# Loading half of the first adjacency block ahead of the class labels in a two-layer graph kernel

## The chip, the cores and the metric

The kernel runs on one core of one Trainium2 chip. The metric is the device time of one execution in microseconds (us). Five engines work side by side and meet through semaphores: TensorE (PE, matrix multiply; PEld is its weight load), VectorE (DVE), ScalarE (ACT), GpSimd (POOL) and SyncE (SP), which here only issues DMAs. Each engine runs its own instructions in order.

## The reference

There are 5000 nodes with 128 features, a symmetric 0/1 adjacency matrix `adj` (5000 x 5000, f32, 100 MB) and one-hot class labels `y` (5000 x 16). Two layers follow, each with a residual and a layer norm:

```
A1   = adj * (y @ y.T);  A1 = A1 / max(row sum of |A1|, 1e-12)
x    = layernorm(x + 0.9 * (A1 @ x) + 0.1 * h0)
sim  = tanh(adj * adj) * (adj > 0);  keep the 350 largest of each row
h2   = tanh(x @ W_proj + b_proj)
x    = layernorm(x + relu(kept @ (h2 @ W_gcn) + b_gcn))
```

So the first layer averages each node's neighbours of the same class. In the second layer every kept entry is tanh(1), as long as no row has more than 350 ones.

## The kernel before

`packed_path` holds the work; `general_path` is a second version that runs only when the data break the first one's assumptions. The 5000 rows are cut into 40 blocks of 128 (the last has 8). Block `t` of `adj` is loaded once, in two halves `h` of 2688 and 2312 columns, into `a_rows[par][h]` (par = t % 2, so two blocks in flight). Each half goes two ways:

- VectorE casts it to 0/1 in bf16 (`cast`, L777, into `a_bits`). TensorE multiplies the bits by powers of two (`pack_rows`, L464), which makes 16-bit words of 16 rows each and turns the block on the way. ScalarE copies the words to `a_words` (L695).
- ScalarE counts its zeros (`count_zeros`, L672), an activation that sums over the row. The counts are for the test of the assumptions at the end.

A half may be overwritten when both are done (SyncE's waits in `load_rows`, L332 and L333). From step 2 on, loads wait for that.

The labels make "words of the same class": ScalarE and VectorE each cast y (L647, L789) and mask it (L649, L791), TensorE transposes (L479) and packs (L488), the results are copied into a block-diagonal form (L655, L797), and `gram_words` (L497) multiplies them. Eight products are made per group, copied into `g_words` by ScalarE and VectorE in turn (`copy_gram`, L317). Then `mask` (L885) takes the AND of a block's adjacency words and class words, `unpack` (L858) spreads the bits into fp8 weights (`turned`), and `multiply` (L527) forms their product with x, which is split into a high and a low f16 part (`high_part` on ScalarE, `low_part` on VectorE). This is the first layer for one block; its norm, projection and `h2 @ W_gcn` follow some steps later, in the same loop.

The loop over blocks is a software pipeline: step t casts, counts and packs block t, masks and unpacks t-1, multiplies t-2, and finishes t-3 to t-7. The first 13 steps are written out; step 0 and 1 have their own order (`first_step`, L950). After the loop over all blocks a second loop multiplies the stored words with the features of the second layer. No `adj` is loaded then.

The order of the start, which the change touches: SyncE issues y in three parts (L350, L351, and L353 after `s_cleared`, a clear by VectorE), then both halves of block 0 (L354), x in six parts, block 1, and the rest. All are on one queue. ScalarE's first data is y (L645), then the diagonal copies and its share of class words; its first count is in step 0 (L715), ahead of the words of block 0 and the high parts of x. VectorE's first data is y (L786); its first cast (L800) comes behind the diagonal copies.

Of the kernel before, what the change touches and what calls it, by code (L numbers as in the profile page):

```python
# [6 lines left out]
P = 128  # L7
# [11 lines left out]
ACT = mybir.ActivationFunctionType  # L19
# [13 lines left out]
HUGE = 2.0 ** 63  # L33
# [3 lines left out]
def packed_path(nc, engines, sem, x, adj, h0, y, w_proj, b_proj, w_gcn, b_gcn, out, flag, s_flag, s_out):  # L37
# [13 lines left out]
    HALF = [slice(0, HB * P), slice(HB * P, N)]  # L51
# [78 lines left out]
    def valid(b):  # L130
        return not isinstance(b, int) or 0 <= b < NB

    with ExitStack() as ctx:
# [158 lines left out]
        def pairs_of(a, lo, hi):  # L292
            return a[lo * P:hi * P, :].rearrange("(s p e) f -> p s (e f)", p=P, e=2)

        def pair_view(t, lo, hi):
            return t[:, lo:hi, :].rearrange("p (s e) f -> p s (e f)", e=2)
# [26 lines left out]

        @engines.sync
        def _(sp):
            def load_rows(t, par, pair):
                if not valid(t):
                    return
                m = rows_of(t)
                for h in range(2):  # L330
                    if not isinstance(t, int) or t >= 2:
                        sp.wait_ge(s_bits, t * 2 - 3 + h)  # L332
                        sp.wait_ge(s_counted, t * 2 - 3 + h)  # L333
                    sp.dma_start(a_rows[par][h][0:m, 0:HALF[h].stop - HALF[h].start],
                                 rows_in(adj, t, par, pair, HALF[h])).then_inc(s_rows[par][h], 16)

            def load_h0(n, par, pair, i, c):

                slot, _ = h0_group(i, c)
                if not isinstance(n, int) or n >= 3:  # L340
                    sp.wait_ge(s_xh, n - 2)
                if isinstance(n, int) and n in (0, LAST):
                    m = rows_of(n)
                    sp.dma_start(h0_rows[slot][0:m, 0, :], rows_in(h0, n, par, pair, slice(0, F))).then_inc(s_h0[slot], 16)
                else:
                    both = h0[P:FULL * P, :].rearrange("(s p e) f -> s p (e f)", p=P, e=2)
                    both = both[pair] if isinstance(n, int) else both[bass.ds(pair, 1), :, :].rearrange("a p c -> p (a c)")
                    sp.dma_start(h0_rows[slot][:, :, :].rearrange("p e f -> p (e f)"), both).then_inc(s_h0[slot], 16)

            sp.dma_start(pair_view(y_nat, 1, FULL), pairs_of(y, 1, FULL)).then_inc(s_in["y"], 16)  # L350
            sp.dma_start(y_nat[:, 0, :], y[0:P, :]).then_inc(s_in["y"], 16)  # L351
            sp.wait_ge(s_cleared, 1)
            sp.dma_start(y_nat[0:TAIL, FULL, :], y[FULL * P:N, :]).then_inc(s_in["yt"], 16)  # L353
            load_rows(0, 0, 0)  # L354
            sp.dma_start(xs[:, 0, :], x[0:P, :]).then_inc(s_in["x0"], 16)
            for q, part in enumerate(X_PART):
                lo, hi = max(part.start, 1), min(part.stop, FULL)
                sp.dma_start(pair_view(xs, lo, hi), pairs_of(x, lo, hi)).then_inc(s_in[f"x{q}"], 16)
            sp.dma_start(xs[0:TAIL, FULL, :], x[FULL * P:N, :]).then_inc(s_in["xt"], 16)
            load_rows(1, 1, 0)  # L360
            load_h0(0, 0, 0, 0, 0)
            load_h0(1, 1, 0, 0, 1)
            sp.dma_start(wp[:, :], w_proj).then_inc(s_in["wp"], 16)
            sp.dma_start(wg[:, :], w_gcn).then_inc(s_in["wg"], 16)
            sp.dma_start(bp_col[:, :], b_proj.rearrange("(p a) -> p a", a=1)).then_inc(s_in["bp"], 16)
            sp.dma_start(bg_row[:, :], b_gcn.rearrange("(a p) -> a p", a=1)).then_inc(s_in["bg"], 16)

            def step(t, par, pair, i, c):
                if not isinstance(t, int) or t >= 2:
                    load_rows(t, par, pair)  # L370
                if valid(t - 1) and c >= 4 and par == 0:
                    load_h0(t - 1, 1, pair - 1, i, c - 1)
            steps4(sp, step, 4, 5)

            def store(t, par, pair):
                m = rows_of(t)
                sp.wait_ge(s_result, t + 1)
                sp.dma_start(rows_in(out, t, par, pair, slice(0, F)), xn[par][0:m, :]).then_inc(s_out[par], 16)
            steps(sp, store, 0)
# [260 lines left out]
        def _(act):  # L640
            act.wait_ge(s_const, 3)
            act.activation(tanh1, ones[:, 0:1], ACT.Tanh).then_inc(s_tanh1, 1)
            act.wait_ge(s_cleared, 2)

            act.wait_ge(s_in["y"], 32)  # L645
            act.wait_ge(s_in["yt"], 16)
            act.activation(y2[:, :, C:2 * C], y_nat[:, :, :], ACT.Copy).then_inc(s_y2, 1)  # L647
# [20 lines left out]
            for g in range(GRAMS):  # L668
                if not gram_on_dve(g):
                    copy_words(g)  # L670

            def count_zeros(t, par, pair, h, m):  # L672


                act.wait_ge(s_rows[par][h], pair * 16 + 16)
                w = HALF[h].stop - HALF[h].start
                col = zeros_in[0:m, bass.ds(t * 2 + h, 1)]
                act.wait_ge(s_counted, t * 2 + h)
                act.activation(count_out[0:m, 0:w], a_rows[par][h][0:m, 0:w], ACT.Relu,  # L679
                               bias=ones[0:m, 0:1], scale=-HUGE,  # L680
                               accum_out=col).then_inc(s_counted, 1)

            def measure(parts, sums, h, n):

# [5 lines left out]
            def step(t, par, pair):  # L690
                odd = (par + 1) % 2

                def words_of(n, par):

                    act.wait_ge(s_packed, n * 2 + 2)  # L695
                    act.activation(at(a_words, n, P).rearrange("p (b w) -> p b w", w=PITCH)[:, :, 0:WORDS + 1],  # L696
                                   words[par][:, 0:NB * PITCH].rearrange("p (b w) -> p b w", w=PITCH)[:, :, 0:WORDS + 1],
                                   ACT.Copy).then_inc(s_words, 1)

                if valid(t - 1) and not (isinstance(t, int) and t <= 1):  # L700
                    words_of(t - 1, odd)
                if isinstance(t, int) and t >= 1:
                    for g in gram_of_step(t - 1):
                        if not gram_on_dve(g):
                            copy_words(g)
                if valid(t - 6):
                    m6 = rows_of(t - 6)
                    act.wait_ge(s_in["bp"], 16)
                    act.wait_ge(s_proj, t - 5)
                    if not isinstance(t, int) or t >= 7:  # L710
                        act.wait_ge(s_feat, t - 6)
                    act.activation(h2_t[:, 0:m6], proj_acc[:, 0:m6], ACT.Tanh, bias=bp_col[:, :])\  # L712
                        .then_inc(s_h2, 1)
                if valid(t):
                    count_zeros(t, par, pair, 0, rows_of(t))  # L715
                if isinstance(t, int) and t == 0:
                    words_of(0, 0)
                    high_part(0)
                    high_part(1)
                    copy_words(GRAMS)  # L720
                    high_part(2)
                    copy_words(GRAMS + 2)
                    high_part(3)
                    copy_words(GRAMS + 4)
                if valid(t - 5):
                    m5 = rows_of(t - 5)
                    act.wait_ge(s_xnt, t - 4)
                    if not isinstance(t, int) or t >= 6:
                        act.wait_ge(s_proj, t - 5)
                    act.activation(xn_t[:, 0:m5], xnt_acc[:, 0:m5], ACT.Copy).then_inc(s_xnt_sb, 1)  # L730
                if valid(t):
                    count_zeros(t, par, pair, 1, rows_of(t))
                if isinstance(t, int) and t == 1:
                    for g in range(2 * GRAMS, 3 * GRAMS):
                        if not gram_on_dve(g):
                            copy_words(g)
                if valid(t - 6):
                    act.wait_ge(s_feat, t - 5)
                    if isinstance(t, int) and t == 6:
                        act.wait_ge(s_cleared, 3)  # L740
                    act.activation(at_cols(f_parts, t - 6, m6, 0, F), feat_acc[0:m6, 0:F], ACT.Copy,
                                   scale=SCALE)\
                        .then_inc(s_high, 1)
# [16 lines left out]
        def _(dve):  # L760
# [16 lines left out]
            def cast(t, par, pair, h):  # L777
# [3 lines left out]
                if not isinstance(t, int) or t >= 1:  # L781
                    dve.wait_ge(s_packed, t * 2 - 1 + h)
                dve.tensor_scalar(a_bits[h][0:m, 0:w], a_rows[par][h][0:m, 0:w], 1.0, None,  # L783
                                  ALU.is_equal).then_inc(s_bits, 1)

            dve.wait_ge(s_in["y"], 32)  # L786
            dve.wait_ge(s_in["yt"], 16)
            dve.wait_ge(s_cleared, 2)
# [7 lines left out]
            for g in range(TURN):  # L796
                dve.tensor_copy(y_diag[g * 2 * C:(g + 1) * 2 * C, Y_PACK[0], g, :],  # L797
                                y_pack[0].rearrange("p (r w) -> p r w", w=GRAM_W)).then_inc(s_yp_sb, 1)

            cast(0, 0, 0, 0)  # L800

            def copy_words(g):
                copy_gram(dve.tensor_copy, dve, g)
# [747 lines left out]
```

## Time and profile before

| | |
|---|---|
| median of 3 runs | 467.72 us (467.58 to 469.69) |
| profiled execution, its own time | 467.99 us |
| its span, first to last instruction | 466.2 us |
| PE / PEld / DVE / ACT / POOL busy | 94 / 83 / 81 / 57 / 34% |
| moved by DMA | 108.50 MB, nearly all before 262 us |

The span is cut into instructions of each engine; a row of a timeline gives start and length, the engine, the line of the program, what is written and read, and in brackets the idle time before it and what ended it. Names such as `a_rows<-in_adj_dram` are out<-in. A DMA is issued by SyncE (SPq, the time there is that of the issue alone) and lands later. The busy share of an engine is an average; only the waits tell what sets the end.

### The profile page before, as it was taken

Reading aid. Unit: us, or ns where it says so; the run is one execution under the profiler, and the core shown is the slowest. Engines: PE = TensorE matmul, PEld = TensorE weight load, DVE = VectorE, ACT = ScalarE, POOL = GpSimd, SP = SyncE. Lnnn points to the kernel's source line nnn. Section 1 sums busy time; section 2 is a strip of 40 time slices with the busy share of each in tenths; the row PEclk is TensorE's granted clock in tenths of the full one; section 3 lists DMA queues with packets and bytes.
Section 4 is the critical chain, followed back from the end, with each engine's and each line's share of the span. In section 5 each row is a group of like instructions: output and inputs, shape, how many; then the busy total and the mean of one; then the engine's idle time right before and its main releaser. Section 6 shows DMA issues by size and latency. Waiting matters only on the chain.

```text
span 466.2 us, 15130 instructions
## 1 busy us (share of the span) xinstructions
PE 437.5 (94%) x5104; PEld 387.8 (83%) x5104; DVE 377.8 (81%) x1358; ACT 263.8 (57%) x355; POOL 160.0 (34%) x310
## 2 busy tenths in 40 slices
PE   3669999999999999999999999999999999999994
PEld 2448988888888988888888887888888888888883
DVE  5988999999999999999999976675576576576562
ACT  4997998989999999999999934900000000000000
POOL 3012543555444455544445541221211221221222
PEclk9987999999999999999999999999999999999999
DMA  8999999999999999999999200000000000000000
GB/s 263 409 414 423 420 419 415 405 389 413 417 419 426 422 422 412 421 424 416 423 417 426 63 2 1 13 11 17 17 11 17 17 11 17 17 11 17 17 12 23
DMA packets 25518, 108.50 MB, mean 233 GB/s; under 512 B 5097, under 2 KB 15490, under 8 KB 15490
## 3 DMA queue, kind: packets, MB, share of 16 engines
q1 hardware_dynamic: 25490, 108.14, 57.4%
q8 instruction: 16, 0.26, 0.2%
q14 instruction: 12, 0.10, 0.1%
HBM read 105.57 MB, written 2.56 MB: 232 GB/s over the span
## 4 chain that ended last, share of the span: by engine, by line
PE 75%; DVE 11%; issue 6%; ACT 5%; DMA 2%; POOL 1%; DVEq 0%; POOLq 0%; SPq 0%; ACTq 0%
PE acc L522 64%; PE words L472 6%; DVE a_bits L783 3%; DMA a_rows<-in_adj_dram 2%; DVE turned L870 2%; PE feat_acc L585 2%; PE proj_acc L596 2%; ACT count_out L679 2%; ACT count_out L686 2%; PE xnt_acc L577 1%; DVE g_words L320 1%; ACT count_out L755 1%; DVE z_high L921 1%; ACT count_out L747 1%; DVE same_class L893 1%
## 5 line engine op out<-in xcount | busy, mean ns | idle before, releaser
L522 PE MATMUL acc<-x_parts,turned 128*128 128x257 f16 (+1 forms) x1600 | 192.9, 277 | 4.8 <-DVE turned L870 3.8
L679 ACT ACTIVATE count_out<-a_rows,ones 128x2688 bf16<-128x2688 f32 (+1 forms) x80 | 190.1, 2377 | 0.5
L522 PEld LDWEIGHTS acc<-x_parts,turned 128*128 128x128 fp8e4 (+1 forms) x1600 | 155.1, 99 | 28.1 <-issue 5.2
L522 PE MATMUL acc<-f_parts,turned 128*128 128x256 f16 (+1 forms) x1560 | 171.6, 273 | 0.8 <-DVE turned L870 0.8
L522 PEld LDWEIGHTS acc<-f_parts,turned 128*128 128x128 fp8e4 (+1 forms) x1560 | 152.0, 98 | 19.2 <-issue 1.3
L783 DVE TENSOR_SCALAR a_bits<-a_rows 128x2688 bf16<-128x2688 f32 (+1 forms) x80 | 116.8, 1460 | 2.4 <-DMA a_rows<-in_adj_dram 2.0
L422 POOL TENSOR_TENSOR var_eps<-mean_var,consts 128x1 f32<-128x1 f32 x80 | 18.5, 232 | 268.0 <-DVE mean_var L1077 139.8
L870 DVE TENSOR_SCALAR turned<-a_words 128x320 uint16 (+1 forms) x305 | 66.5, 232 | 53.6 <-PE acc L522 53.2
L425 POOL TENSOR_TENSOR rstd<-var_eps,consts 128x1 f32<-128x1 f32 x80 | 86.4, 1080 | 6.3
L870 DVE TENSOR_SCALAR turned<-same_class 128x320 uint16<-128x320 uint16 x313 | 71.1, 253 | 0.1
L472 PEld LDWEIGHTS words<-pack,a_bits 128*128 128x128 bf16 (+1 forms) x1600 | 51.6, 97 | 9.3 <-DVE a_bits L783 7.4
L472 PE MATMUL words<-pack,a_bits 128*128 128x9 bf16 (+1 forms) x1600 | 52.0, 167 | 6.1 <-DVE a_bits L783 6.1
L882 DVE TENSOR_SCALAR xn<-z,mean_var,rstd 128x128 f32<-128x128 f32 x79 | 32.5, 412 | 2.7 <-POOL rstd L425 0.9
L411 POOL TENSOR_TENSOR h_part<-h_rows,consts 128x128 f32<-128x128 f32 (+1 forms) x40 | 21.9, 548 | 20.4 <-DMA h_rows<-in_L_gnn_h_dram 20.3
L696 ACT ACTIVATE a_words<-words 128x360 f32 (+1 forms) x40 | 18.9, 472 | 15.5 <-PE words L472 15.4
L439 POOL COPY xs<-xn 128x128 f32 (+2 forms) x40 | 23.6, 590 | 0.5 <-DVE xn L882 0.5
L416 POOL TENSOR_TENSOR xh<-h_part,xs 128x128 f32<-128x128 f32 (+1 forms) x40 | 21.2, 529 | 6.5 <-POOL h_part L411 5.6
L1053 DVE SCALAR_TENSOR_TENSOR low_feat<-acc,consts,bg_all 128x128 f32<-128x128 f32 (+1 forms) x40 | 13.7, 344 | 4.7 <-PE acc L522 4.7
L712 ACT ACTIVATE h_t<-proj_acc,bp_col 128x128 f32<-128x128 f32 (+1 forms) x40 | 14.4, 360 | 5.1 <-PE proj_acc L596 5.1
L585 PE MATMUL feat_acc<-wg,h_t 128*128 128x128 f32 (+1 forms) x80 | 15.6, 277 | 0.8 <-ACT h_t L712 0.6
L730 ACT ACTIVATE xn_t<-xnt_acc 128x128 f32<-128x128 f32 (+1 forms) x40 | 10.9, 273 | 9.0 <-PE xnt_acc L577 8.6
L596 PE MATMUL proj_acc<-xn_t,wp 128*128 128x128 f32 (+1 forms) x80 | 15.5, 275 | 0.2 <-issue 0.2
(110 smaller groups left out, 288.1 us busy)
## 6 DMA issues: line engine op xcount, KB each, us to landing
a_rows<-in_adj_dram SPq DMA_DIRECT2D x39, 1344.0 KB, 7.9
a_rows<-in_adj_dram SPq DMA_DIRECT2D x39, 1156.0 KB, 8.3
out_dram<-xn SPq DMA_DIRECT2D x39, 64.0 KB, 1.5
h_rows<-in_L_gnn_h_dram SPq DMA_DIRECT2D x19, 128.0 KB, 8.0
xs<-in_x_dram SPq DMA_DIRECT2D x3, 640.0 KB, 10.2
xs<-in_x_dram SPq DMA_DIRECT2D x1, 512.0 KB, 9.0
y_nat<-in_L_gnn_y_dram SPq DMA_DIRECT2D x1, 304.0 KB, 3.6
a_rows<-in_adj_dram SPq DMA_DIRECT2D x1, 84.0 KB
```

The lines of the kernel that those rows point to most:

```text
L411: pool.tensor_tensor(h0_part[0:m, :], h0_rows[slot][0:m, h0_place(c), :], alpha[0:m, :].to_broadcast([m, F]), ALU.mult).then_inc(s_h0part, 1)
L416: pool.tensor_tensor(xh[par][0:m, :], h0_part[0:m, :], at(xs, n, m), ALU.add)\
L425: pool.tensor_tensor(rstd[par][0:m, :], var_eps[0:m, :], neg_half[0:m, :], ALU.pow)\
L439: pool.tensor_copy(at(xs, t - 4, m), xn[par][0:m, :]).then_inc(s_kept, 1)
L472: mm = pe.matmul(words[par][:, b * PITCH:b * PITCH + WORDS + 1], a_bits[h][0:m, c:c + (P - 1) * d + 1:d], pack[0:m, :], start=True, stop=True)
L522: mm = pe.matmul(acc[par][0:m, 0:cols], bits, parts[:, b, 0:cols], start=first and b == blocks[0], stop=last and b == blocks[-1])
L585: pe.matmul(feat_acc[0:m6, 0:F], h2_t[:, 0:m6], wg[:, :], start=True, stop=True)\
L596: pe.matmul(proj_acc[:, 0:m5], wp[:, :], xn_t[:, 0:m5], start=True, stop=True)\
L679: act.activation(count_out[0:m, 0:w], a_rows[par][h][0:m, 0:w], ACT.Relu, bias=ones[0:m, 0:1], scale=-HUGE, accum_out=col).then_inc(s_coun ...
L783: dve.tensor_scalar(a_bits[h][0:m, 0:w], a_rows[par][h][0:m, 0:w], 1.0, None, ALU.is_equal).then_inc(s_bits, 1)
L870: up = dve.tensor_scalar(turned_at(n, par)[:, :, bit * WORDS:(bit + 1) * WORDS], source, abs(shift), ONE_PAIR, op, ALU.bitwise_and)
L882: return dve.tensor_scalar(xn[par][0:m, :], z[par][0:m, :], mean_var[par][0:m, 0:1], rstd[par][0:m, :], ALU.subtract, ALU.mult)
```

## The change

`load_rows` gets an argument that picks halves. The first half of block 0 is issued as the very first DMA, y behind it, and the second half where both were. `count_zeros` moves up in ScalarE's program and its first call stands ahead of the wait for y; VectorE's first cast stands ahead of its wait for y. Amounts of work and of data stay the same.

```diff
@@ engines.sync
-            def load_rows(t, par, pair):
+            def load_rows(t, par, pair, halves=(0, 1)):
...
-                for h in range(2):
+                for h in halves:
...
+            load_rows(0, 0, 0, (0,))
             sp.dma_start(pair_view(y_nat, 1, FULL), pairs_of(y, 1, FULL)).then_inc(s_in["y"], 16)
             sp.dma_start(y_nat[:, 0, :], y[0:P, :]).then_inc(s_in["y"], 16)
             sp.wait_ge(s_cleared, 1)
             sp.dma_start(y_nat[0:TAIL, FULL, :], y[FULL * P:N, :]).then_inc(s_in["yt"], 16)
-            load_rows(0, 0, 0)
+            load_rows(0, 0, 0, (1,))
@@ engines.scalar
+            def count_zeros(t, par, pair, h, m):
...
+            count_zeros(0, 0, 0, 0, P)
             act.wait_ge(s_in["y"], 32)
             act.wait_ge(s_in["yt"], 16)
...
-                if valid(t):
+                if valid(t) and not (isinstance(t, int) and t == 0):
                     count_zeros(t, par, pair, 0, rows_of(t))
@@ engines.vector
+            cast(0, 0, 0, 0)
             dve.wait_ge(s_in["y"], 32)
...
-
-            cast(0, 0, 0, 0)
```

## Rows read from the trace of the kernel before

**Rows 1.** Windows: stretch, its length, busy us by engine, granted clock, DMA share, GB/s.
```profile
core 0: us, PE busy (x) PEld busy (x) DVE busy (x) ACT busy (x) POOL busy (x), PEclk, DMA share, GB/s
35.00:49.00 14.00, 14.00 (x165) 11.63 (x166) 11.85 (x38) 11.59 (x13) 3.93 (x8) 0.80 1.02 424
49.00:101.00 52.00, 50.24 (x699) 45.42 (x696) 51.58 (x157) 48.31 (x67) 23.23 (x38) 1.00 1.00 407
101.00:258.00 157.00, 153.72 (x2130) 139.72 (x2131) 155.16 (x477) 146.76 (x201) 78.84 (x126) 1.00 1.01 419
```
**Rows 2.** The chain of waits in order of time: start us, length us, what.
```profile
39.23 9.63 DMA a_rows<-in_adj_dram
```
**Rows 3.** Timeline of SyncE's issues: start us, length us, line, out<-in.
```profile
0.75 0.44 SPq L350 DMA_DIRECT2D y_nat<-in_L_gnn_y_dram  x1
1.25 1.53 SPq L351 DMA_DIRECT2D y_nat<-in_L_gnn_y_dram  x1
2.84 0.37 SPq L353 DMA_DIRECT2D y_nat<-in_L_gnn_y_dram  x1
3.25 0.82 SPq L334 DMA_DIRECT2D a_rows<-in_adj_dram  x2
...
17.09 0.33 SPq L334 DMA_DIRECT2D a_rows<-in_adj_dram  x1
```
**Rows 4.** Issues to landing, us: y, block 0's first half, then all loads until 30.
```profile
y_nat<-in_L_gnn_y_dram SPq DMA_DIRECT2D x1, 304.0 KB, 3.6
...
a_rows<-in_adj_dram SPq DMA_DIRECT2D x1, 1344.0 KB, 6.2
...
DMA to landing us min/median/max: 6.2/8.7/12.9
```
**Rows 5.** Windows: DMA at the start.
```profile
1.70:3.60 1.90, 0.00 (x0) 0.00 (x0) 0.43 (x1) 0.53 (x2) 1.33 (x9) 1.00 1.06 166
3.50:6.00 2.50, 0.00 (x0) 0.00 (x0) 0.65 (x5) 0.95 (x2) 1.86 (x13) 1.00 0.73 190
```
**Rows 6.** Timeline of VectorE at the start.
```profile
10.14 1.56 DVE L783 TENSOR_SCALAR a_bits<-a_rows 128x2688 bf16<-128x2688 f32 x1
...
12.21 0.68 DVE L320 CAST g_words<-proj_acc 128x512 uint16<-128x512 f32 x1
12.81 1.35 DVE L783 TENSOR_SCALAR a_bits<-a_rows 128x2312 bf16<-128x2312 f32 x1
```
**Rows 7.** Timeline of ScalarE at the start.
```profile
4.86 0.74 ACT L647 ACTIVATE f_parts<-y_nat 128x640 bf16<-128x640 f32 x1 [2.62 <-DMA y_nat<-in_L_gnn_y_dram]
...
12.66 2.53 ACT L679 ACTIVATE count_out<-a_rows,ones 128x2688 bf16<-128x2688 f32 x1
...
15.18 0.46 ACT L696 ACTIVATE a_words<-words 128x360 uint16<-128x360 f32 x1
...
21.61 2.24 ACT L679 ACTIVATE count_out<-a_rows,ones 128x2312 bf16<-128x2312 f32 x1
```
**Rows 8.** Timeline of TensorE at the start.
```profile
6.56 0.69 PE L479 MATMUL proj_acc<-ident_b,f_parts 128*128 128x128 bf16 x5 [6.56 <-DVE f_parts L789]
...
11.08 0.63 PE L504 MATMUL proj_acc<-y_diag,y_t 128*128 128x256 bf16 x2
...
19.66 6.49 PE L522 MATMUL acc<-x_parts,turned 128*128 128x257 f16 x40 [0.44 <-DVE x_parts L810]
```
**Rows 9.** Timeline of VectorE from 35 to 49 us.
```profile
35.94 1.56 DVE L783 TENSOR_SCALAR a_bits<-a_rows 128x2688 bf16<-128x2688 f32 x1 [1.22 <-DMA a_rows<-in_adj_dram]
...
44.09 0.32 DVE L893 TENSOR_TENSOR same_class<-a_words,g_words 128x320 uint16<-128x320 uint16 x1 [0.43 <-ACT a_words L696]
...
48.89 1.81 DVE L783 TENSOR_SCALAR a_bits<-a_rows 128x2688 bf16<-128x2688 f32 x1 [0.73 <-DMA a_rows<-in_adj_dram]
```
**Rows 10.** Timeline of ScalarE: the words of block 3.
```profile
43.59 0.47 ACT L696 ACTIVATE a_words<-words 128x360 uint16<-128x360 f32 x1 [2.21 <-PE words L472]
```
**Rows 11.** Timeline of TensorE: the same 21 matmuls twice.
```profile
35.49 4.70 PE L522 MATMUL acc<-x_parts,turned 128*128 128x257 f16 x21
...
43.41 2.47 PE L522 MATMUL acc<-x_parts,turned 128*128 128x257 f16 x21
```

More of the change, by code:

```diff
@@ L643, in _ @@
             act.wait_ge(s_cleared, 2)
+            def count_zeros(t, par, pair, h, m):
+                act.wait_ge(s_rows[par][h], pair * 16 + 16)
+                w = HALF[h].stop - HALF[h].start
+                col = zeros_in[0:m, bass.ds(t * 2 + h, 1)]
+                act.wait_ge(s_counted, t * 2 + h)
+                act.activation(count_out[0:m, 0:w], a_rows[par][h][0:m, 0:w], ACT.Relu,
+                               bias=ones[0:m, 0:1], scale=-HUGE,
+                               accum_out=col).then_inc(s_counted, 1)
+            count_zeros(0, 0, 0, 0, P)
             act.wait_ge(s_in["y"], 32)
@@ L670, in _ @@
                     copy_words(g)
[L672 to L681, printed above, removed]
             def measure(parts, sums, h, n):
```

## The prediction, made before the changed kernel was run

> **What bounds the kernel now.** I first read busy time, clock and DMA by stretch. From 101 us on TensorE and VectorE are both busy about 98% of the time, and from 49 to 101 us VectorE alone is (51.58 of 52.00 us) [rows 1]. In those stretches nothing stands idle that could give a late start back: whatever the kernel is behind at 49 us stays, and whatever it is ahead stays too. So the question is what the change does to the first 49 us. There the chain of waits passes through one load of adjacency rows of 9.63 us, which ends at 48.86 us [rows 2]. VectorE has idled for it 0.73 us before its cast at 48.89 us [rows 9]. So at 49 us the DMA stream leads the engines by only 0.73 us, and there are two ways to move the end: move the stream, or move the engines by more than that. The share of the DMA engines is 1.02 between 35 and 49 us, so the stream itself is full there [rows 1].
>
> Next I read the orders of SyncE, VectorE, ScalarE and TensorE at the start [rows 3, 6, 7, 8]. Everything is issued on SyncE's one queue. The labels y are issued at 0.75 us and ScalarE starts on them at 4.86 us. From y comes a long chain: two casts, transposes on TensorE at 6.56 us, block-diagonal copies, the words of equal class, their copies on VectorE (12.21 us), the cast of the second half of block 0 (12.81 us), the mask and the low parts of x, and at 19.66 us the first product. All of it is in order on engines with hardly a hole, so a delay at its head runs through.
>
> **The DMA order.** Before, the first half of block 0 (1344 KB) is issued at 3.25 us and lands 6.2 us later, at 9.4 us; y lands 3.6 us after its issue at 0.75 us, at 4.35 us [rows 3, 4]. After, the half is issued at 0.75 us, on an empty queue as before (y's packets are through by 3.6 us and the traffic between 3.5 and 6.0 us is 190 GB/s, not the 420 of later) [rows 1, 5]. I take the same 6.2 us: it lands at 6.95 us. y is queued behind it. Its packets begin when those of the half are through. The last y transfers of before were through at about 3.6 us and the engine started on y at 4.86 us, so packets end some 1.2 us before use; for the half take 0.9 us before landing, 6.05 us. y then needs its 1.9 us of packets [rows 5], until 7.95 us, and can be used at 9.15 us. Against 4.86 us that is 4.3 us late. (SyncE's second y issue takes 1.53 us, a stall until the first is in the queue [rows 3]. It will now stall until about 7 us, and the tail of y and the second half of the block are issued after it, at 7.1 and 7.5 us, just as y drains. Before, that half was second in line behind 1344 KB; now it is second behind the same bytes. So the rest of the stream stands where it stood: gain or loss 0; at best it gains what the hole between 3.5 and 6.0 us is worth, (420-190) GB/s x 2.5 us = 575 KB = 1.4 us; at worst it loses the 0.5 us of a new hole.)
>
> The Trainium skill, DMA: Bandwidth & Descriptors, section Anatomy of one DMA, gives for one DMA (of the path through GpSimd) about 2.0 us fixed plus its bytes at 436 GB/s. By it, as an estimate, the half lands 5.2 us after its issue, where the row has 6.2. The trace doesn't agree for this first big transfer; the measurement decides. By the page everything in the next paragraph would come 1.0 us earlier and the end with it.
>
> **The cast and the count.** The cast of that half (10.14 us, 1.56 us long) goes to 6.95-8.5 us, before y can be used at 9.15: VectorE hides it wholly [rows 6]. The count (12.66 us; the next ScalarE work came at 15.18, so 2.52 us) runs from 6.95 to 9.5 us [rows 7]. Behind it on ScalarE is queued its cast of y, which starts at 9.5 instead of 4.86 us and takes 0.74 us; TensorE's transposes wait for it. Before they waited for VectorE's cast and started 0.25 us after it. So they start at 10.24+0.25 = 10.5 us instead of 6.56: 3.9 us late [rows 8].
>
> What gives some of it back: VectorE no longer has 1.56 us of cast between the diagonal copies and the copies of words. The words in proj_acc start at 11.08 us on TensorE and take 0.63 us; 3.9 us later they end at 15.6 us, and VectorE copies them then instead of at 12.21 us: 3.4 us late [rows 6, 8]. The cast of the second half follows directly (12.81 to 16.2 us), and the whole chain from there (words of block 0, mask, unpack, low parts, first product 19.66 to 23.1 us) moves by the same 3.4 us. On ScalarE the count of 2.5 us is out of the way, but the words of block 0 that it copies at 15.18 us [rows 7] hang on the same cast, so the high parts of x are late too and the second count moves from 21.61 to about 25.0 us. Bounds for this shift: 2.4 us if the half lands after 5.2 us (the 1156 KB half takes 2.8 us of packets at 420 GB/s, the 1344 KB half 3.3, and latency of y 1.0+1.2 us on top), and 3.9 us if nothing is given back; I take 3.4.
>
> **What is absorbed.** Casting block 3 at 35.94 us, VectorE had idled 1.22 us for a transfer [rows 9]. It loses that wait, so VectorE is 3.4-1.2 = 2.2 us late there. But TensorE is not helped. Its first product of the second block starts at 35.49 us, and from there it has no idle time until 49 us (14.00 us busy of 14.00) [rows 1, 11]. It is 3.4 us late, so ScalarE's words of block 3, for which it already waits 2.21 us at 43.59 us, come 3.4 us late, and the mask at 44.09 us with them [rows 9, 10]. The next slack is the 0.73 us at 48.89 us. So at 49 us: 3.4-0.73 = 2.7 us late. TensorE is behind by the full 3.4 us, which VectorE's pace hides later: TensorE has 1.76 us idle between 49 and 101 us, VectorE 0.42 us [rows 1]. I take off 0.1 us for the latter: **2.6 us**.
>
> **Do loads starve?** SyncE issues the load of block 2's second half only after the second count, which ends at 23.84 us before and at about 27.2 us after. The load ahead of it, issued at 17.09 us, lands 12.9 us later, at 30.0 us [rows 3, 4]. So the queue holds work until about 29 us, and the late issue costs nothing. The same holds for the chain's transfer: its issue moves from 39.23 to 42.6 us, and the transfer before it ends about 9.63-3.4 = 6.2 us after 39.23, at 45.4 us. If the cover were gone, each microsecond of hole would cost up to one, less the lateness of the engines.
>
> **The sum.** The profiled execution took 467.99 us with a span of 466.2 us. 467.99+2.6 = 470.6 us; the median of the three runs is 467.72, 0.27 below it, so 470.3 us.
>
> **The rivals.**
> 1. Faster, y hardly delayed. If the small packets of y get through beside the big ones, or the half is through in little more than 1344 KB at 420 GB/s = 3.3 us, so that y isn't the later of the two, the chain loses the 1.56 us of cast and gains. Then the stream sets the time at 49 us, and it is ahead by the hole of 1.4 us [rows 5]: 467.7-1.4 = 466.3 us. It decides from the point where y can be used before 6.4 us (4.86+1.56). For it: the hole is there, VectorE and ScalarE idle until 4.86 us. Against: one queue, and y's packets before were through before the first byte of the half counted.
> 2. The delay is half absorbed by TensorE's clock. The 21 matmuls at 35.49 us took 4.70 us, the same 21 at 43.41 us 2.47 us; the granted clock means 0.80 between 35 and 49 us, a mix of the 1.2 and 2.4 GHz levels [rows 1, 11]. If after the shift these 21 find the high clock, TensorE is 3.4-2.2 = 1.2 us late and VectorE 3.4-1.2 = 2.2 at its cast of block 4, of which the 0.43 us before the mask at 44.09 and the 0.73 us after it are slack: 2.2-0.43-0.73 = 1.0 us, 468.8 us. The Trainium skill, TensorE: Matmul & The Clock Gate, Part 1: The HAM clock gate, says that the moment of a change of level isn't tied to the kernel's start and differs between runs; no second trace of before shows that here. Against it, the low stretch in the trace follows TensorE's idling, which moves with the chain.
> 3. Starved loads. With issues 3.4 us late and a new hole of 0.5 us after y, blocks 3 to 5 land late; a cost of 1.5 us more than forecast, 471.8 us. Against it: the margins above.
> 4. The change does what it says but the start isn't on the path: 467.7 us. Against it are the 14.00 us of TensorE without idle time.
>
> **Chances.** Forecast 0.50 (own range 469.4 to 471.3), rival 2 0.20, rival 4 0.08, rival 1 0.12, rival 3 0.10. The measurement can tell about 0.5%, 2.3 us, from no change, so the bounds are 465.4 and 470.06 us. Above 470.06: two thirds or more of the forecast (0.36), rival 3, and a little of rival 2: 0.48. Faster by over 0.5%: less than half of rival 1 and nothing else, since it must find 2.3 us: 0.07. The rest, 0.45, within. The range goes from 466.8, which cuts off most of rival 1, to 471.9 us.
>
> **What would show it.** In the profile after: the first load issued at about 0.75 us and landing near 7 us; the second y issue stalled for several microseconds; ScalarE's count ahead of its cast of y, which starts at 9 to 10 us; first transposes near 10.5, first product near 23 us; no wait of VectorE for rows before the casts near 36 us and 49 us; the cast of block 5's first half at 51.5 instead of 48.89 us; and from there the same pace. I am wrong if y can be used before 7 us, if the first product starts within 1 us of 19.66, or if the late start is there and the cast of block 5 isn't late.

## The result, and the profile after

The changed kernel takes 470.53 us (median of 9 runs, 470.06 to 470.96) against 467.77 us before (9 runs beside them): the ratio is 1.005, 95% interval 1.0038 to 1.0061. It is slower by 2.8 us by the medians, and by 2.3 us by the ratio. The forecast was 470.3 us. The profiled execution was the fastest of the nine, 470.06 us with a span of 468.3 us, 2.1 us above the span before. One execution of experiment 5 (637.31 us) and one of experiment 8 (745.06 us) ran at a mean granted clock of 0.66 and 0.58, against 0.99 in the others, and are left out below.

SyncE's issues, timeline of the changed kernel (start us, length us), then the time from issue to landing of block 0's first half, of the large part of y, and of the second half:

```profile
0.76 0.39 SPq L334 DMA_DIRECT2D a_rows<-in_adj_dram  x1
1.21 0.42 SPq L351 DMA_DIRECT2D y_nat<-in_L_gnn_y_dram  x1
1.67 5.05 SPq L352 DMA_DIRECT2D y_nat<-in_L_gnn_y_dram  x1
6.77 0.38 SPq L354 DMA_DIRECT2D y_nat<-in_L_gnn_y_dram  x1
7.19 0.35 SPq L334 DMA_DIRECT2D a_rows<-in_adj_dram  x1
...
a_rows<-in_adj_dram SPq DMA_DIRECT2D x1, 1344.0 KB, 5.9
...
y_nat<-in_L_gnn_y_dram SPq DMA_DIRECT2D x1, 304.0 KB, 7.1
...
a_rows<-in_adj_dram SPq DMA_DIRECT2D x1, 1156.0 KB, 5.5
```

The half lands at 6.7 us and y's large part at 8.3 us instead of at 4.35 [rows 4]. The second y issue stalls for 5.05 us, where it stalled for 1.53 [rows 3], so the second half is issued only at 7.19 us and lands at 12.7 us. ScalarE at the start, changed kernel:

```profile
6.75 2.54 ACT L653 ACTIVATE count_out<-a_rows,ones 128x2688 bf16<-128x2688 f32 x1 [4.51 <-issue]
...
9.29 0.72 ACT L660 ACTIVATE f_parts<-y_nat 128x640 bf16<-128x640 f32 x1
...
18.08 0.47 ACT L698 ACTIVATE a_words<-words 128x360 uint16<-128x360 f32 x1 [1.71 <-PE words L473]
...
24.51 2.24 ACT L653 ACTIVATE count_out<-a_rows,ones 128x2312 bf16<-128x2312 f32 x1
```

The cast of y starts at 9.29 us against 4.86 [rows 7], directly behind the count. The count now runs at the start, and the time that it leaves free further on turns into a wait of 1.71 us for the words of block 0. TensorE, changed kernel:

```profile
10.15 0.69 PE L480 MATMUL proj_acc<-ident_b,f_parts 128*128 128x128 bf16 x5 [10.15 <-ACT f_parts L660]
...
22.81 7.19 PE L523 MATMUL acc<-x_parts,turned 128*128 128x257 f16 x40 [0.69 <-DVE x_parts L811]
...
39.11 3.81 PE L523 MATMUL acc<-x_parts,turned 128*128 128x257 f16 x21
```

Against [rows 8] the transposes are 3.59 us late and the first product 3.15 us. The 21 matmuls of block 1 start 3.62 us late but take 3.81 us, not 4.70 [rows 11]. VectorE, changed kernel:

```profile
6.70 1.56 DVE L785 TENSOR_SCALAR a_bits<-a_rows 128x2688 bf16<-128x2688 f32 x1 [0.95 <-DMA a_rows<-in_adj_dram]
8.80 0.49 DVE L792 CAST f_parts<-y_nat 128x640 bf16<-128x640 f32 x1 [0.54 <-DMA y_nat<-in_L_gnn_y_dram]
...
15.35 0.69 DVE L320 CAST g_words<-proj_acc 128x512 uint16<-128x512 f32 x1 [0.16 <-PE proj_acc L505]
15.95 1.36 DVE L785 TENSOR_SCALAR a_bits<-a_rows 128x2312 bf16<-128x2312 f32 x1
...
38.25 1.55 DVE L785 TENSOR_SCALAR a_bits<-a_rows 128x2688 bf16<-128x2688 f32 x1
...
46.75 0.32 DVE L894 TENSOR_TENSOR same_class<-a_words,g_words 128x320 uint16<-128x320 uint16 x1 [0.64 <-ACT a_words L698]
...
50.79 1.56 DVE L785 TENSOR_SCALAR a_bits<-a_rows 128x2688 bf16<-128x2688 f32 x1
```

Both waits for rows of [rows 9] are gone: the casts of block 3 (2.31 us late) and of block 5 (1.90 us late) follow without one, and the mask between them is 2.66 us late. From there nothing is given back: the end is 2.1 us late. By stretch, changed kernel (columns as in [rows 1]):

```profile
34.00:40.00 6.00, 3.42 (x51) 2.41 (x50) 5.92 (x14) 5.84 (x7) 0.00 (x0) 0.59 0.93 341
35.00:49.00 14.00, 12.38 (x169) 10.21 (x170) 13.23 (x42) 12.79 (x12) 2.82 (x4) 0.76 0.99 380
49.00:101.00 52.00, 50.67 (x704) 45.95 (x701) 51.22 (x157) 49.01 (x68) 24.59 (x40) 1.00 1.01 412
101.00:258.00 157.00, 153.61 (x2129) 139.45 (x2127) 155.16 (x477) 146.65 (x201) 78.13 (x125) 1.00 1.01 420
```

After 49 us VectorE and TensorE are as full as in [rows 1]. Between 35 and 49 us TensorE has 1.62 us of idle time where it had none, since its work starts later, and the DMA stream has thinned from 424 to 380 GB/s.

### The profile page after: what moved, and what is told of

Same layout as the page of the kernel before. It is cut to its first block, busy times and chain, and to the rows that moved or that the text cites. A ratio compares the mean times of both kernels' runs of the same rounds, so it can differ in the third digit from the quotient of the medians.

```text
span 468.3 us, 15130 instructions
## 1 busy us (share of the span) xinstructions
PE 437.1 (93%) x5104; PEld 387.5 (83%) x5104; DVE 377.8 (81%) x1358; ACT 263.6 (56%) x355; POOL 162.2 (35%) x310
## 4 chain that ended last, share of the span: by engine, by line
PE 77%; DVE 11%; issue 6%; ACT 4%; POOL 2%; DMA 0%; DVEq 0%; POOLq 0%; ACTq 0%
PE acc L523 65%; PE words L473 6%; DVE a_bits L785 4%; DVE turned L871 2%; PE feat_acc L586 2%; PE proj_acc L597 2%; ACT count_out L688 2%; PE xnt_acc L578 1%; DVE g_words L320 1%; ACT count_out L757 1%; DVE z_high L922 1%; POOL rstd L426 1%; ACT count_out L749 1%; ACT count_out L653 0%; DVE same_class L894 0%
## 5 line engine op out<-in xcount | busy, mean ns | idle before, releaser
L412 POOL TENSOR_TENSOR h_part<-h_rows,consts 128x128 f32<-128x128 f32 (+1 forms) x40 | 23.8, 595 | 21.3 <-DMA h_rows<-in_L_gnn_h_dram 21.1
L440 POOL COPY xs<-xn 128x128 f32 (+2 forms) x40 | 24.9, 623 | 0.5 <-DVE xn L883 0.5
L417 POOL TENSOR_TENSOR xh<-h_part,xs 128x128 f32<-128x128 f32 (+1 forms) x40 | 20.1, 502 | 6.5 <-POOL h_part L412 5.6
L586 PE MATMUL feat_acc<-wg,h_t 128*128 128x128 f32 (+1 forms) x80 | 15.6, 277 | 0.8 <-ACT h_t L714 0.6
L732 ACT ACTIVATE xn_t<-xnt_acc 128x128 f32<-128x128 f32 (+1 forms) x40 | 10.9, 274 | 8.9 <-PE xnt_acc L578 8.7
L597 PE MATMUL proj_acc<-xn_t,wp 128*128 128x128 f32 (+1 forms) x80 | 15.5, 275 | 0.2 <-issue 0.2
```

The source lines that it names most:

```text
L412: pool.tensor_tensor(h0_part[0:m, :], h0_rows[slot][0:m, h0_place(c), :], alpha[0:m, :].to_broadcast([m, F]), ALU.mult).then_inc(s_h0part, 1)
L417: pool.tensor_tensor(xh[par][0:m, :], h0_part[0:m, :], at(xs, n, m), ALU.add)\
L440: pool.tensor_copy(at(xs, t - 4, m), xn[par][0:m, :]).then_inc(s_kept, 1)
L586: pe.matmul(feat_acc[0:m6, 0:F], h2_t[:, 0:m6], wg[:, :], start=True, stop=True)\
L597: pe.matmul(proj_acc[:, 0:m5], wp[:, :], xn_t[:, 0:m5], start=True, stop=True)\
```

## The experiments

All times are medians beside runs of the kernel before on the same chip; the interval is that of the ratio. Twelve kernels ran; together they vary when the chain of y starts and what causes it. "First product" is TensorE's first product with x (19.66 us before), "transposes" its first work on y (6.56 us before).

**1. Only the order of the DMAs.** SyncE as in the changed kernel, ScalarE and VectorE as before.

```diff
+            load_rows(0, 0, 0, (0,))
             sp.dma_start(pair_view(y_nat, 1, FULL), ...)
...
-            load_rows(0, 0, 0)
+            load_rows(0, 0, 0, (1,))
```

> The half of block 0 is issued ahead of y, but its cast and its count stay where they were before the change. Theory (the late y is what costs): y can be used near 8.8 us as in the changed kernel; ScalarE casts it at once instead of at 9.29 us, so TensorE's transposes start near 9.7 us instead of 10.15; but VectorE has the 1.56 us of cast again between the diagonal copies and the copies of words, so the first product comes at 22.8 to 23.5 us (22.81 in the changed kernel) and the time is 470.3 to 471.5 us. Rival (the moved count, which keeps ScalarE from y, is what costs): first product near 20 us, time within 0.5 us of before.

470.36 us against 467.75, 1.0059 (1.0045 to 1.0072). Transposes at 9.79 us, first product 22.89 us. The order of the loads alone brings the whole loss, and the rival, that the moved count is what costs, falls.

**2. Only the computation moved.** The changed kernel with the DMA order of before.

```diff
-            load_rows(0, 0, 0, (0,))
...
-            load_rows(0, 0, 0, (1,))
+            load_rows(0, 0, 0)
```

> The DMA order of before, with the cast and the count of the first half ahead of the work on y. Both engines then wait for rows that land at 9.4 us although y is there at 4.9. Theory: count 9.4 to 11.9 us, ScalarE's cast of y at 11.9, transposes at 12.8 (6.2 us late), first product near 25.2 us; less the 0.73 us by which the stream led, and some tenths for VectorE's missing cast: +4.5 to +5.5 us, 472.3 to 473.3 us. Rival (only the order of the DMAs matters): no change, 467.8 us.

474.22 us, 1.0145 (1.0128 to 1.0162); y's cast on ScalarE at 11.82 us, transposes 12.68, first product 25.32. The direction is the theory's and the rival falls; the size is a microsecond above its range (four executions, 472.53 to 475.12). The two parts of the change don't add. Alone, this one holds y until the rows have landed and been counted (9.28 to 11.82 us). Together with the new order the rows are there at 6.7 us, the count ends at 9.29, hardly after y can be used at 8.80, and the transposes are 3.59 us late instead of 6.12.

**3. The count back in its old place**, the rest as changed.

```diff
-            count_zeros(0, 0, 0, 0, P)
...
-                if valid(t) and not (isinstance(t, int) and t == 0):
+                if valid(t):
```

> The changed kernel, but ScalarE's first count goes back behind the class words, to where it was; the cast of the half stays ahead. Theory (the lateness of y, not the count, makes nearly all of it): transposes start near 9.7 instead of 10.15 us, 0.5 us earlier; the count of 2.5 us fills ScalarE's wait of 1.71 us before the words of block 0 and puts these 0.4 us later than that gain; first product 22.6 to 23.3 us; time within 0.5 us of the changed kernel's 470.5. Rival (the count ahead of y is the cost): time back to 468.5 us or less.

470.46 us, 1.0056 (1.0043 to 1.007): as the changed kernel. Transposes at 9.77, first product 22.41 us, 0.2 us ahead of the expected range and 0.40 us ahead of the changed kernel. That doesn't show in the time: the count ahead of y costs nothing measurable, since most of it runs while y is on its way anyway.

**4. A long delay of the chain, loads untouched.** The kernel before, with copies on ScalarE ahead of its cast of y.

```diff
+            act.activation(count_out[:, 0:2688], ones[:, 0:1].to_broadcast([P, 2688]), ACT.Copy).then_inc(s_delay, 1)
+            act.wait_ge(s_delay, 1)
+            (the same with 1536 columns, wait for 2)
             act.activation(y2[:, :, C:2 * C], y_nat[:, :, :], ACT.Copy).then_inc(s_y2, 1)
```

> The kernel before, DMA order and all, with two idle copies of 2688 and 1536 columns on ScalarE just ahead of its cast of y: about 4.1 us more on ScalarE there, which starts the transposes about 3.4 us late (ScalarE's cast ended 0.7 us before it was needed). They compute nothing that is used. Theory (a late start of the class words passes through whole, less the 0.73 us lead at 48.89 us and what the clock gives back): +2.0 to +2.8 us, 469.8 to 470.6 us, though every load is issued as before. Rival (the change costs by what it does to the DMA stream: the second half lands 0.42 us late, loads are issued late): within 0.5 us of before.

471.04 us, 1.0066 (1.0053 to 1.008). Transposes at 9.74, first product 22.84 us, within 0.1 us of experiment 1. With the loads of the start in the order of before, the loss is the same. So a late start of the work on y is enough for the whole loss, whatever the change does to the rows. The time came out above the expected range, and the VectorE timeline shows where some of the rest is:

```profile
45.28 1.56 DVE L788 TENSOR_SCALAR a_bits<-a_rows 128x2688 bf16<-128x2688 f32 x1 [0.58 <-DMA a_rows<-in_adj_dram]
...
51.63 1.56 DVE L788 TENSOR_SCALAR a_bits<-a_rows 128x2688 bf16<-128x2688 f32 x1 [0.70 <-DMA a_rows<-in_adj_dram]
```

VectorE waits for rows again, 0.58 us at block 4 and 0.70 us at block 5, and the cast of block 5 is 2.74 us late here, 1.90 in the changed kernel. A late count frees its buffer late, and the first half of block 4 is issued at 37.20 us instead of 33.28. But the changed kernel issues it as late, at 37.12 us, without a wait: there it lands 6.5 us after its issue, here 8.1. The stream has fallen behind earlier, with 352 GB/s between 28 and 34 us against 421 in the changed kernel. Why it did is not shown.

**5. A short delay.** The same with one copy of 1920 columns:

```diff
+            act.activation(count_out[:, 0:1920], ones[:, 0:1].to_broadcast([P, 1920]), ACT.Copy).then_inc(s_delay, 1)
+            act.wait_ge(s_delay, 1)
             act.activation(y2[:, :, C:2 * C], y_nat[:, :, :], ACT.Copy).then_inc(s_y2, 1)
```

> The kernel before with one idle copy of 1920 columns (about 1.9 us) on ScalarE ahead of its cast of y, which starts the transposes about 1.2 us late; every load as before. The long delay (transposes 3.18 us late, time +3.29 us) took both leads of the stream that the trace before shows (1.22 us at 35.94 and 0.73 us at 48.89 us), or lost them again. Theory (the stream leads by 0.73 us, the rest passes): +0.3 to +0.8 us, 468.0 to 468.6 us. Rival (every delay at the head passes whole, there is no lead): +1.2 us or more, 469.0 us.

468.57 us against 467.67, 1.0014 (1.0005 to 1.0023): +0.65 us by the ratio, +0.9 by the medians, for transposes and first product 1.06 us late. The interval is 0.2 to 1.1 us, so it excludes the rival's 1.2 us but not a full 1.06 us, and the times alone decide little. The trace (468.17 us) shows the swallowing itself:

```profile
36.06 1.56 DVE L786 TENSOR_SCALAR a_bits<-a_rows 128x2688 bf16<-128x2688 f32 x1 [0.45 <-DMA a_rows<-in_adj_dram]
...
49.12 1.55 DVE L786 TENSOR_SCALAR a_bits<-a_rows 128x2688 bf16<-128x2688 f32 x1
```

The wait for the rows of block 3 is 0.45 instead of 1.22 us and that for block 5 is gone; the two casts are 0.12 and 0.23 us late, and the span is 0.2 us longer.

**6. Both halves ahead of y**, computation as before.

```diff
+            load_rows(0, 0, 0)
             sp.dma_start(pair_view(y_nat, 1, FULL), ...)
...
-            load_rows(0, 0, 0)
```

> Both halves of block 0 are issued ahead of y; casts and counts stand where they were before the change. Theory (the time follows the lateness of the transposes, whatever makes it): the second half lands near 9.9 us, y's 1.9 us of packets follow, y can be used near 11.8 us, transposes near 12.7 us, 6.1 us late. The kernel with the computation alone moved had them 6.1 us late too and took 474.2 us: 473.3 to 474.7 us. Rival (earlier rows give part of it back, so that the cost of the order levels off): below 472.5 us.

473.74 us, 1.0139 (1.0115 to 1.0163); transposes 12.58, first product 25.68 us. The cost doesn't level off. Having 2500 KB of rows there at 9.8 us gives nothing back that shows in the time.

**7 and 8. y on a queue of its own.** ScalarE issues y's three DMAs as its first instructions, while SyncE starts with the rows; once on the kernel before and once on the changed one.

```diff
 def _(act):
+            act.dma_start(pair_view(y_nat, 1, FULL), pairs_of(y, 1, FULL)).then_inc(s_in["y"], 16)
+            act.dma_start(y_nat[:, 0, :], y[0:P, :]).then_inc(s_in["y"], 16)
+            act.wait_ge(s_cleared, 1)
+            act.dma_start(y_nat[0:TAIL, FULL, :], y[FULL * P:N, :]).then_inc(s_in["yt"], 16)
```

> The kernel before with y's three DMAs issued from ScalarE's queue at the same time as block 0's rows from SyncE's. Cast and count stand where they were before. Theory: the two queues share the 16 DMA engines, so y is slowed but doesn't wait for the whole half; y can be used between 5.5 and 7.5 us and the rows' second half lands 0.7 to 1.4 us earlier than 12.2 us, since SyncE is never held by y. Time between 467.0 us (y by 5.5) and 469.0 us (y at 7.5), since each microsecond of y beyond some 0.7 us costs one. Rival (y on its own queue gets no share while big packets flow): y after 8 us, 470 us.

> The changed kernel (cast and count ahead of y) with y's three DMAs issued from ScalarE's queue. The rows land no earlier than 6.7 us, and the count holds ScalarE until 9.3 us, whenever y lands. Theory: transposes at 10.1 us as in the changed kernel, so 470.1 to 470.8 us, though y lands 1 to 3 us earlier. Rival (only y's landing matters): 468.5 us or less.

478.48 us, 1.0233 (1.022 to 1.0246), and 479.42 us, 1.0254 (1.0241 to 1.0267). Both expectations missed by 8 us or more; only the first one's rival, that y gets no share and lands after 8 us, had the direction. y's large part takes 15.5 us to land and ScalarE casts y at 17.11 us in both. The DMA view of the first kernel between 9 and 16 us (q1 is SyncE's queue, q10 ScalarE's; packets, MB, share) and ScalarE's row:

```profile
q1 hardware_dynamic: 2211, 2.19, 88.4%
q10 hardware_dynamic: 2209, 0.27, 25.4%
...
y_nat<-in_L_gnn_y_dram ACTq DMA_DIRECT2D x1, 304.0 KB, 15.5
```
```profile
17.11 0.74 ACT L648 ACTIVATE f_parts<-y_nat 128x640 bf16<-128x640 f32 x1 [4.52 <-DMA y_nat<-in_L_gnn_y_dram]
```

The queues take turns packet by packet, 2211 to 2209. y's packets have 128 bytes and x's 1024; while the rows flowed, with 10752 bytes a packet, it was one small for one big, 341 to 339 between 3.5 and 9 us. The turns are single packets: in the three tenths of a microsecond from 4.4 us on the two queues have 3 and 3, 5 and 5, 3 and 3, and with several packets of y in a row on one engine, at 13 ns each, such short pieces would hold uneven numbers. A transfer of many small packets gets an equal share of the turns, not of the bytes. The Trainium skill, DMA: Bandwidth & Descriptors, section Queues, rings and completion order, says that each engine goes round its queues packet by packet, which these rows show; it adds that a packet has some 9 to 17 descriptors as a rule, and by the rows the turn here is a single 128-byte one.

**9. The small pieces of y first, the large one third**, then the rows.

```diff
-            (the large part of y)
             sp.dma_start(y_nat[:, 0, :], y[0:P, :]).then_inc(s_in["y"], 16)
             sp.wait_ge(s_cleared, 1)
             sp.dma_start(y_nat[0:TAIL, FULL, :], y[FULL * P:N, :]).then_inc(s_in["yt"], 16)
+            (the large part of y)
             load_rows(0, 0, 0)
```

> The kernel before, but the two small pieces of y are issued first and the large one third, directly ahead of block 0's rows, so that SyncE stands at most at the rows' issue while y is pushed. Theory: y can be used some 0.3 us earlier (its tail is no longer last), and the first rows follow y without the hole near 3.75 us, so half a microsecond less of the stream is lost; both the chain of y and the stream gain 0.3 to 0.5 us, so the time is 467.3 to 467.5 us, 0.2 to 0.5 us faster than before. It also shows whether the slow first row packets (0.9 us each against 0.4 later) come with an empty queue: then they are at full speed here and the stream gains 1 us or more. Rival: no difference, 467.75 us.

467.62 against 467.67 us, 0.9996 (0.9987 to 1.0005): no difference, where 0.2 to 0.5 us were expected. y was usable later, at 5.42 us instead of 4.86, since its large part started later, but the transposes stood at 6.56 us as before, since VectorE casts y only at 5.70 us in the kernel before, behind the packing weights. So y had some 0.8 us to spare there. And the first row packets followed y without a hole and were slow all the same.

**10. The chain of y started earlier.** VectorE's cast of y ahead of the operations on the packing weights, on the kernel before.

```diff
+            (the three waits and the cast of y)
             dve.wait_ge(s_pack, BITS)
             dve.memset(pack[:, WORDS:WORDS + 1], 1.0)
...
-            (the three waits and the cast of y)
```

> The kernel before, with VectorE's cast of y ahead of the small operations on the packing weights, for which it waits until 5.3 us. TensorE's transposes start 0.5 to 0.7 us earlier (near 5.9 us) and so does the chain behind them. Theory (before, the stream of rows sets the time at 48.89 us, and the engines have 0.73 us of slack there): the gain turns into a longer wait for rows, near 1.4 us, and the time stays within 0.15 us of before. Rival (the chain is the bound on both sides): 0.5 to 0.7 us faster, 467.1 us.

467.63 against 467.86 us, 0.9999 (0.999 to 1.0008), though the transposes start at 5.76 us, 0.80 us earlier. VectorE waits for rows in its place:

```profile
30.07 1.56 DVE L787 TENSOR_SCALAR a_bits<-a_rows 128x2688 bf16<-128x2688 f32 x1 [0.58 <-DMA a_rows<-in_adj_dram]
...
32.86 1.37 DVE L787 TENSOR_SCALAR a_bits<-a_rows 128x2312 bf16<-128x2312 f32 x1 [0.26 <-DMA a_rows<-in_adj_dram]
...
36.05 1.56 DVE L787 TENSOR_SCALAR a_bits<-a_rows 128x2688 bf16<-128x2688 f32 x1 [1.22 <-DMA a_rows<-in_adj_dram]
...
48.43 1.56 DVE L787 TENSOR_SCALAR a_bits<-a_rows 128x2688 bf16<-128x2688 f32 x1 [0.41 <-DMA a_rows<-in_adj_dram]
```

Two new waits, 0.58 and 0.26 us, take up the 0.8 us: the cast of block 3 is at 36.05 us, 0.11 us later than before. The time is as the theory had it, the place of the wait is not: it expected some 1.4 us at block 5, where the wait is 0.41 us and the cast 0.46 us early. This execution is the fastest of its eleven (467.23 us). So up to 36 us the stream of rows is the bound on the early side, and the chain of y on the late side; the kernel before stood near the bend.

**11 and 12. The weights' loads deferred** behind block 4's rows, alone and with experiment 10.

```diff
-            sp.dma_start(wp[:, :], w_proj).then_inc(s_in["wp"], 16)
-            sp.dma_start(wg[:, :], w_gcn).then_inc(s_in["wg"], 16)
...
+                if isinstance(t, int) and t == 4:
+                    (the same two)
```

> The kernel before, with the loads of the two weight matrices (64 KB each, 0.3 us of the stream at 420 GB/s) issued after block 4's rows instead of ahead of block 2's. Theory: rows of blocks 2 to 4 land 0.3 us earlier; block 5's wait at 48.89 us stays, since the weights' bytes are then behind block 4, so the time gains 0 to 0.3 us: 467.4 to 467.7 us. Rival (no part of the time hangs on the stream): no change at all and the casts at 30.15, 35.94 and 42.07 us where they were.

> Both of the last two edits. Theory: chain and stream are both earlier, so this gains more than either alone, 0.2 to 0.5 us: 467.2 to 467.5 us. Rival: the sum of nothing and nothing, 467.7 us.

467.92 and 467.94 us against 467.86, 1.0001 (0.9993 to 1.001) and 0.9999 (0.9991 to 1.0008). Both expectations (a gain of up to 0.3 us, and of 0.2 to 0.5) missed, though a gain of 0.3 us would hardly show in intervals of 0.4 us to each side. In the trace of the first, the fastest of its eleven executions, the casts of blocks 3 and 4 are 0.34 and 0.35 us early, as expected, and that of block 5 is 0.50 us early; in that of the second these are 0.3 to 0.5 us late. So that an earlier stream would gain time is not shown. Nothing here beats the kernel before.

## Why the prediction was right, step by step

The prediction has two steps: what the late y does to the first product, and what of that is left at the cast of block 5 near 49 us, behind which nothing is given back. All kernels of this document, by the traces and by the times:

| kernel | transposes late by | first product late by | cast of block 5 late by | span longer by | time by the ratio |
|---|---|---|---|---|---|
| chain earlier (10) | -0.80 us | -0.56 us | -0.46 us | -0.8 us | 0.0 us |
| weights deferred (11) | 0.02 | 0.02 | -0.50 | -0.5 | 0.0 |
| both of these (12) | -0.70 | -0.50 | 0.30 | 0.2 | 0.0 |
| small pieces first (9) | 0.00 | 0.00 | -0.13 | -0.2 | -0.2 |
| short delay (5) | 1.06 | 1.06 | 0.23 | 0.2 | +0.7 |
| count late (3) | 3.21 | 2.75 | 2.34 | 2.5 | +2.6 |
| **changed kernel** | 3.59 | 3.15 | 1.90 | 2.1 | +2.3 |
| long delay (4) | 3.18 | 3.18 | 2.74 | 3.0 | +3.1 |
| order only (1) | 3.23 | 3.23 | 2.92 | 3.3 | +2.8 |
| computation only (2) | 6.12 | 5.66 | 4.71 | 4.5 | +6.8 |
| both halves first (6) | 6.02 | 6.02 | 5.37 | 5.0 | +6.5 |
| y on its own queue (7) | 11.43 | 11.43 | 10.26 | 10.1 | +10.9 |
| the same, changed kernel (8) | 11.43 | 10.98 | 10.26 | 10.2 | +11.9 |

The columns up to the span are of one profiled execution each. In every one the span is longer by what the cast of block 5 is late, within 0.4 us, so the premise holds that what the kernel is behind at 49 us stays. Between the first product and that cast 0.3 to 1.3 us of a delay are swallowed. The times by the ratio are of all executions and go with the lateness of the first product within about a microsecond to either side: 0.8 us below it for the changed kernel, 1.1 us above it for experiment 2. That scatter is not explained by these columns.

- *The half's landing* was taken as 6.2 us after issue; 5.9 was measured. Right, 0.3 us high, and this carries through: y usable at 8.80 instead of 9.15 us, transposes at 10.15 instead of 10.5, the copy of class words at 15.35 instead of 15.6, the first product at 22.81 instead of 23.1. The estimate of 5.2 us from the Trainium skill, DMA: Bandwidth & Descriptors, section Anatomy of one DMA, lies further from this 5.9 us than the row of before.
- *"ScalarE's cast of y behind the count"*: right (9.29 us, forecast 9.5). But the count matters less than the text made it seem: experiment 3 took it away and the time stayed. y itself was there only at 8.8 us.
- *What is given back*: forecast 0.5 us between transposes and first product (3.9 to 3.4); measured 0.44.
- *"TensorE is not helped"*: half right. It started the second block's product 3.62 us late (forecast 3.4), but part of rival 2 came true: those matmuls met the higher clock for a part of their run, 3.81 us against 4.70, and the mask was 2.66 us late instead of 3.4. In experiment 1 they did not. The matmuls, and the granted clock while they ran (PEclk, third from the right), of experiment 1 and then of the changed kernel:

```profile
22.89 6.91 PE L523 MATMUL acc<-x_parts,turned 128*128 128x257 f16 x40 [0.44 <-DVE x_parts L811]
...
38.90 4.69 PE L523 MATMUL acc<-x_parts,turned 128*128 128x257 f16 x21
...
38.90:43.59 4.69, 4.69 (x29) 3.33 (x28) 4.60 (x17) 4.60 (x7) 0.28 (x2) 0.50 0.95 359
```
```profile
39.11:42.92 3.81, 3.81 (x29) 2.88 (x29) 3.73 (x12) 3.72 (x7) 0.00 (x0) 0.64 0.98 398
```

  A mean of 0.50 is the 1.2 GHz level throughout, as it was before from 34 to 40 us; 0.64 has some of the 2.4 GHz level in it. In experiment 1 the cast of block 5 came 2.92 us late and that execution took 471.25 us, 1.2 us more than the profiled one of the changed kernel, with the first product at the same place within 0.1 us. Among the fourteen traces of this document the same 21 matmuls took 4.7 us in nine, 3.8 in three (the changed kernel and experiments 2 and 4) and 4.3 and 4.5 in the other two. Profiles of the other executions don't exist, so how often the changed kernel has the one or the other is open. By the trace the forecast was too high by 0.5 us (470.6 for the profiled execution, which took 470.06), and by the medians 0.2 us too low (470.3 against 470.53). The median agrees better than the mechanism does: the profiled execution had 0.9 us given back by the clock, which the forecast left out, and how far the other eight had it is not known. So that agreement may be luck in part.
- *The two leads of the stream*, 1.22 and 0.73 us: right. Both waits are gone, the first helps VectorE alone, and from the mask to the cast of block 5 the lateness falls from 2.66 to 1.90 us, by 0.76.
- *"The rest of the stream stands where it stood"*: roughly right for the wrong reason. There was no hole worth the name behind y, but the slow start of big packets was paid twice (below), so the second half landed 0.4 us later, at about 12.7 instead of 12.2 us.
- *"The late issue costs nothing"*: wrong in its argument. The queue did run thin: 341 GB/s between 34 and 40 us in the changed kernel, where the same stretch before had 419. It cost nothing in the changed kernel, where the engines were as late as the rows. In experiment 4, with the loads issued as late, VectorE did wait, 0.58 and 0.70 us: rival 3, in small.
- *Rival 1* (y hardly delayed) falls with y's landing at 8.3 us, 1.6 us behind the half's. Its variant with queues side by side is experiment 7, and it went the other way by 11 us. *Rival 4* (the start isn't on the path) falls with experiments 4 and 6.
- *y's lateness*: forecast 4.3 us, measured 3.9 (usable at 8.80 us against 4.86). Of it 0.8 us were to spare before (experiment 9), so that in experiments 1 and 3 the transposes are 3.2 us late, and the count on ScalarE adds about 0.4 in the changed kernel.

## What to carry to other kernels

Before moving a load ahead of another on one queue, ask which of the two has the longer chain behind it: the one that heads a long serial chain goes first, even if it is small and makes inefficient packets, and filling the idle start of an engine with other work isn't a gain if that work's data push the chain's data back. When a kernel is at the bend between a stream and a chain, an earlier start of the chain alone bought nothing measurable (experiment 10) while a later one cost most of its length; read both slacks before spending either. Don't put a transfer of many small packets on a queue beside one with large packets if a long chain waits for it.

## What the runs showed of the hardware

- When big row packets start after y, or at the very beginning, the first microsecond and a quarter is slow: 215 and 185 GB/s, against 419 and 396 in full flow. The DMA in the changed kernel, by stretch: from 1.75 us (the first half), in full flow, at the second half's start, and in full flow again.

```profile
1.75:3.00 1.25, 0.00 (x0) 0.00 (x0) 0.38 (x1) 0.48 (x2) 0.87 (x6) 1.00 1.02 215
3.25:5.25 2.00, 0.00 (x0) 0.00 (x0) 0.00 (x0) 0.00 (x0) 1.43 (x10) 1.00 0.99 419
8.00:9.25 1.25, 0.00 (x0) 0.00 (x0) 0.71 (x3) 1.25 (x2) 0.00 (x0) 1.00 0.95 185
9.50:11.25 1.75, 1.10 (x10) 0.99 (x10) 0.62 (x2) 1.23 (x2) 0.00 (x0) 1.00 0.97 396
```

  It isn't an empty queue: in experiment 9 the rows follow y directly and the stretch is as slow.

```profile
4.25:5.25 1.00, 0.00 (x0) 0.00 (x0) 0.00 (x0) 0.00 (x0) 0.71 (x6) 1.00 1.14 210
```

  Nor is it every transfer's: in experiment 6 the second half follows the first directly and flows at full rate.

```profile
6.00:8.50 2.50, 0.00 (x0) 0.00 (x0) 0.00 (x0) 0.00 (x0) 0.00 (x0) 1.00 1.00 422
```

  Its cause stays open. In the changed kernel it is paid twice.
- The issue of a DMA right behind y's large part (2432 packets of 128 bytes) stands until a good part of these packets is through, so it also stands for everything that lies ahead of them: 1.53 us on SyncE before, 5.05 us behind block 0's half, 9.18 us on ScalarE in experiment 7, for 8 KB each time. When it ended, some 1250, 1400 and 790 small packets had started. Everything that the engine has to do behind it stands too; ScalarE's table load of 1.28 us started at 11.1 us there.
